# A fused attention and mixture-of-experts block on one core: expert weights in nine loads, block rows turned on VectorE, and a rewritten closing section

## The reference

```
gate = ki @ w0; hb = ki @ w2; hidden = silu(gate) * hb          # per head
w1g = newtonschulz5((hidden * lr1)^T vi)    # w0g, w2g alike: two rounds of X @ X^T, A @ A, B @ X
w_  = normalized(w_ + w_g)
oi  = silu(qi @ w0) * (qi @ w2) @ w1
```

```
gup = xf @ gate_up_proj[e] + 2 * (xf @ A^T) @ B^T               # 512 -> 2 * 256
h   = silu(gates) * h
out = h @ down_proj[e] + 2 * (h @ dA^T) @ dB^T                  # 256 -> 512
y   = sum of the two selected experts, weighted
```

## Time and profile before

| | us |
|---|---|
| median of 3 runs | 909.91 |
| the runs | 909.87, 912.17, 909.91 |
| the profiled execution, its own time | 913.66 |
| its span | 911.9 |
| PE / DVE / ACT busy | 849.4 / 646.5 / 644.4 |
| steady loop, one block | 5.81 |

### The profile page before, as it was taken

One profiled execution on the slowest core, in us unless ns is written; L12 is line 12 of the kernel. 1 busy time (PEld: TensorE's weight loads), 2 busy tenths in 40 slices (PEclk: granted clock), 3 DMA queues, 4 the chain that ended last, 5 costly groups with the idle time before them and its releaser, 6 DMA issues.

```text
span 911.9 us, 16072 instructions
## 1 busy us (share of the span) xinstructions
PE 849.4 (93%) x5128; PEld 525.9 (58%) x5128; DVE 646.5 (71%) x2315; ACT 644.4 (71%) x1417; POOL 347.0 (38%) x285
## 2 busy tenths in 40 slices
PE   6999999999999999999999999998899989999994
PEld 3657576575766757566575765756554434444442
DVE  2798989899898988989889898989735322222221
ACT  2878988888888988988888888887733323333331
POOL 2334344454444445344454444443132322222222
PEclk9999999999999999999999999999799999999998
DMA  9766426163351624426053250437334553444540
GB/s 329 269 208 175 117 93 176 49 195 88 123 148 66 206 60 150 117 93 187 23 164 102 85 140 19 111 92 296 158 72 70 125 92 62 84 84 80 84 73 0
DMA packets 56082, 110.98 MB, mean 122 GB/s; under 512 B 6576, under 2 KB 8240, under 8 KB 55360
## 3 DMA queue, kind: packets, MB, share of 16 engines
q1 hardware_dynamic: 47680, 92.84, 33.9%
q0 software_dynamic: 8176, 16.85, 9.8%
q10 hardware_dynamic: 144, 0.26, 0.1%
HBM read 47.22 MB, written 64.55 MB: 123 GB/s over the span
## 4 chain that ended last, share of the span: by engine, by line
PE 68%; DVE 14%; ACT 8%; DMA 4%; POOL 3%; issue 3%; SPq 0%; DVEq 0%; ACTq 0%; POOLq 0%
PE bank L128 17%; PE bank L134 10%; PE bank L1100 9%; PE bank L1121 5%; POOL t_small L2925 2%; PE bank L604 2%; PE bank L697 2%; DVE t_small L1598 2%; ACT t_arena L2506 1%; PE bank L641 1%; PE bank L609 1%; PE bank L636 1%; PE bank L627 1%; PE bank L677 1%; DMA xs_scratch<-t_arena 1%
## 5 line engine op out<-in xcount | busy, mean ns | idle before, releaser
L128 PEld LDWEIGHTS bank<-t_arena 128*128 128x128 bf16 (+1 forms) x1536 | 123.7, 123 | 112.7 <-issue 30.7
L128 PE MATMUL bank<-t_arena 128*128 128x128 bf16 (+1 forms) x1536 | 157.3, 238 | 16.0 <-ACT t_arena L2515 6.4
L134 PE MATMUL bank<-t_ident,t_arena 128*128 128x128 f32 x618 | 99.4, 282 | 14.0 <-DVE t_arena L1156 6.1
L134 PEld LDWEIGHTS bank<-t_ident,t_arena 128*128 128x128 f32 x618 | 72.3, 143 | 64.9 <-issue 37.8
L1100 PE MATMUL bank<-t_arena 128*128 x200 | 90.2, 594 | 2.4 <-ACT t_arena L2856 2.4
L3076 POOL DMA_INDIRECT out_x<-t_arena,t_tokx x25 | 38.6, 1546 | 111.7 <-DVE t_small L2226 101.6
L2847 ACT ACTIVATE t_arena<-bank 128x256 f32<-128x256 f32 x25 | 9.6, 383 | 78.0 <-PE bank L1100 78.0
L2229 DVE TENSOR_TENSOR t_arena<-t_arena,bank 128x256 f32<-128x256 f32 x25 | 10.5, 421 | 76.3 <-ACT t_arena L2847 76.3
L2931 POOL TENSOR_TENSOR t_small<-t_small,t_half 128x8 f32<-128x8 f32 x14 | 24.4, 1746 | 103.5 <-DVE t_small L1598 103.5
L1100 PEld LDWEIGHTS bank<-t_arena 128*128 128x128 f32 x200 | 35.9, 189 | 38.8 <-issue 38.8
L128 PE MATMUL bank<-t_W,t_arena 128*128 128x128 f32 x384 | 53.4, 282 | 0.7 <-ACT t_W L2416 0.2
(11 more groups left out here) (1097 smaller groups left out, 2322.9 us busy)
## 6 DMA issues: line engine op xcount, KB each, us to landing
xs_scratch<-t_arena SPq DMA_DIRECT2D x16, 2064.0 KB
t_arena<-xs_scratch SPq DMA_DIRECT2D x39, 258.0 KB, 2.7
t_arena<-in_gate_up SPq DMA_DIRECT2D x32, 256.0 KB, 3.6
wm_scratch<-t_arena SPq DMA_DIRECT2D x30, 256.0 KB
t_arena<-wm_scratch SPq DMA_DIRECT2D x5, 1536.0 KB, 11.0
t_arena<-in_wmod SPq DMA_DIRECT2D x5, 1024.0 KB, 10.4
t_arena<-in_down SPq DMA_DIRECT2D x16, 256.0 KB, 3.1
out_x<-t_arena SPq DMA_DIRECT2D x16, 256.0 KB, 2.0
```

The costliest lines, as they stand in the source:

```text
L128: mm = pe.matmul(bank[:, s], lhs[:, s], rhs[:, s], start=True, stop=True)
L134: mm = pe.transpose(bank[:, 128 * k:128 * k + 128], src[:, 128 * k:128 * k + 128], idn)
```

## The change

1. **Weights.** `expert(e, lo, hi)` loads part of an expert. There are nine transfers (four of 2048 columns, four of 1024, one of 3072). Three of 2048 columns stand ahead of chunk 14's output store on SP, each behind the last reader of its place: the products of chunk 14, and `m03`, `m13` of chunk 15's preparation. Block 0's "up" now waits for `s_e` 144.
2. **Rows.** `rows_in` loads a block in five transfers in place of one: four of 32 partitions x 4 pieces of 128 values (512 bytes each), which put the 32x32 squares where they belong, and one of 128x4 for the number, expert and weights (`xq`). DVE turns all sixteen squares in one instruction, and reads each square's columns four values apart; ACT reads SBUF, not a bank, for `xT`. PE's four transposes of each block are gone. The columns of the gate, the low-rank and the up weights are permuted outside the kernel to fit, so that the result is the same. `APPLY`'s transposes of h2 stay on PE, and take every fourth column (`h2k`).
3. **Order.** Chunk 15's section is written in a new order on all engines: the count of tokens per expert, its table and the output products of chunk 14 come first, chunk 15's forward products after them; up(0) to up(3) stand among the Newton-Schulz steps; up(13) stands before T(12); chunk 15's scatter stands behind block 8's in place of block 6's.

The core of the diff:

```
-        xg = cut(34820, 516, RING)
-        fs = cut(37916, 256, 2)
+        xg = cut(34820, 512, RING)
+        xgk = [r.rearrange("p (b i k) -> p b k i", b=4, k=4) for r in xg]
+        fs = cut(37892, 256, 2)
+        xr = arena[:, 38404:38916]
+        squares = xr.rearrange("p (b k j) -> p b k j", b=4, k=4)
...
-                turned(pe, A1, h2x, 4, ident[:, :]).then_inc(apply_pe, 1)
+                for k in range(4):
+                    mm = pe.transpose(A1[:, 128 * k:128 * k + 128], h2k[:, k, :], ident[:, :])
+                mm.then_inc(apply_pe, 1)
...
-                if t < NB:
-                    pe.wait_ge(s_g[t % RING],16 * (t // RING + 1))
-                    if t >= 1:
-                        pe.wait_ge(tn_act, nth(TN_ACT, t-1, "xT"))
-                    turned(pe, P0, xg[t % RING], 4, ident[:, :]).then_inc(tn_pe, 1)
...
-                    dve.wait_ge(s_g[t % RING],16 * (t // RING + 1))
+                    dve.wait_ge(s_g[t % RING],80 * (t // RING + 1))
+                    if t >= 1:
+                        dve.wait_ge(tn_act, nth(TN_ACT, t-1, "xT"))
+                    dve.transpose(xr, xgk[t % RING]).then_inc(tn_dve, 1)
...
+            def rows_in(sp, t, at):
+                for a in range(4):
+                    src = xs[bass.ds(at, 128), 128 * a:128 * a + 128].rearrange("(b j) n -> j b n", j=32)
+                    sp.dma_start(xg[t % RING][32 * a:32 * a + 32, :].rearrange("j (b n) -> j b n", b=4), src).then_inc(s_g[t % RING], 16)
+                sp.dma_start(xq[t % RING], xs[bass.ds(at, 128), 512:516]).then_inc(s_g[t % RING], 16)
...
             for c in range(NC - 1):
+                if c == NC - 2:
+                    sp.wait_ge(s_ms, 16 * STORED[NC - 1])
+                    for sem in (n0_pe, n1_pe, n2_pe):
+                        sp.wait_ge(sem, nth(N0_PE, c, "G"))
+                    sp.wait_ge(fwd_pe, len(FWD_PE) * (NC - 1))
+                    expert(7, 0, 2048)
+                    sp.wait_ge(prep_pe, nth(PREP_PE, NC - 1, "m03"))
+                    expert(0, 0, 2048)
+                    sp.wait_ge(prep_pe, nth(PREP_PE, NC - 1, "m13"))
+                    expert(2, 0, 2048)
```

And the head of the closing section on PE:

```
+            pe.wait_ge(mg_dve, nth(MG_DVE, NC - 2, "u0"))
+            pe.matmul(P0[:, 0:8], onesb[:, :], cum[(NC - 2) % 2][:, :], start=True, stop=True).then_inc(ta_pe, 1)
+            heads(pe, A0, W[0], qT[0]).then_inc(apply_pe, 1)
+            heads(pe, A1, W[2], qT[0]).then_inc(apply_pe, 1)
+            heads(pe, B0, kT[1], W[0]).then_inc(fwd_pe, 1)
```

More of the change, by code:

```diff
@@ L275, in adaln_block @@
         wx = [sm(1) for _ in range(RING)]
+        xq = [sm(4) for _ in range(RING)]
         full, ends, step8, done, rem, last = [sm(NE) for _ in range(6)]
@@ L962, in _ @@
             mm.then_inc(dn_pe, 1)
+            pe.wait_ge(apply_dve, nth(APPLY_DVE, NC - 1, "h2"))
+            for k in range(4):
+                mm = pe.transpose(A1[:, 128 * k:128 * k + 128], h2k[:, k, :], ident[:, :])
+            mm.then_inc(apply_pe, 1)
             pe.wait_ge(tn_act, nth(TN_ACT, 7, "xT"))
@@ L970, in _ @@
             turned(pe, CC(6), fs[0], 2, ident[:, :]).then_inc(dn_pe, 1)
-            pe.wait_ge(s_g[2], 32)
-            turned(pe, P0, xg[8 % RING], 4, ident[:, :]).then_inc(tn_pe, 1)
+            pe.wait_ge(apply_act, nth(APPLY_ACT, NC - 1, "h2T"))
+            for k in range(4):
+                q = slice(32 * k, 32 * k + 32)
+                mm = pe.matmul(A0[q, 0:128], gwm[:, k, :], h2T[:, 128 * k:128 * k + 128], start=True, stop=True)
+            mm.then_inc(apply_pe, 1)
             pe.wait_ge(dn_act, nth(DN_ACT, 6, "fT"))
@@ L1065, in _ @@
             mm.then_inc(dn_pe, 1)
-            pe.wait_ge(tn_act, nth(TN_ACT, NC - 3, "xT"))
-            for k in range(4):
-                mm = pe.matmul(AA(13)[:, :], xT[1][:, 128 * k:128 * k + 128],
-                               w_e[:, bass.ds(which[13], 1), 512 * k:512 * k + 512], start=(k == 0), stop=(k == 3))
-            mm.then_inc(up_pe, 1)
             pe.wait_ge(up_dve, nth(UP_DVE, NC - 3, "fs"))
@@ new lines, in _ @@
+            dve.tensor_tensor(last, ends, full, ALU.subtract).then_inc(tab_dve, 1)
+            dve.wait_ge(s_g[0], 240)
+            dve.wait_ge(tn_act, nth(TN_ACT, 11, "xT"))
+            dve.transpose(xr, xgk[12 % RING]).then_inc(tn_dve, 1)
+            dve.tensor_scalar(tokx[12 % RING], xq[12 % RING][:, 0:1].bitcast(U32), 2047, None, ALU.bitwise_and).then_inc(tn_dve, 1)
+            dve.tensor_scalar(wx[12 % RING], xq[12 % RING][:, 1:2], ebf[:, 12:12 + 1], xq[12 % RING][:, 2:3], ALU.is_equal, ALU.mult).then_inc(tn_dve, 1)
@@ L2638, in _ @@
-            act.wait_ge(n2_pe, nth(N2_PE, NC - 1, "AA0"))
-            act.copy(NTT[2], B2[:, :]).then_inc(n2_act, 1)
+            act.wait_ge(n2_pe, nth(N2_PE, NC - 1, "BX0"))
+            act.copy(NZT[2], B2[:, :]).then_inc(n2_act, 1)
+            act.wait_ge(tn_dve, nth(TN_DVE, 0, "tr"))
+            for k in range(4):
+                row = act.activation(xT[0][:, 128 * k:128 * k + 128].rearrange("p (b j) -> p b j", b=4), squares[:, :, k, :], ACT.Identity, scale=cb_c[:, k:k + 1], bias=sb_c[:, k:k + 1])
@@ L2842, in _ @@
                     act.copy(fT[b % 2], CC(b)[:, 0:256]).then_inc(dn_act, 1)
+                if t < NB:
+                    act.wait_ge(tn_dve, nth(TN_DVE, t, "tr"))
+                    if t >= 2:
+                        act.wait_ge(up_pe, nth(UP_PE, t-2, "up"))
+                    if t == 0:
+                        act.wait_ge(apply_pe, nth(APPLY_PE, NC - 2, "hq"))
+                    for k in range(4):
+                        row = act.activation(xT[t % 2][:, 128 * k:128 * k + 128].rearrange("p (b j) -> p b j", b=4), squares[:, :, k, :], ACT.Identity, scale=cb_c[:, k:k + 1], bias=sb_c[:, k:k + 1])
+                    row.then_inc(tn_act, 1)
                 if EB <= u < NB:
```

1354 lines of the change are left out of this document (666 added, 688 removed).

## The result

Twenty executions of each: 911.97 us median before, 908.55 us after; the ratio of the two is 0.997 with a 95% interval of 0.9958 to 0.9983, so 1.5 to 3.8 us faster. The forecast was 16.2 us faster, and the time lies outside 886 to 902.

The account below looks back on a forecast made before the run. PE's own work was taken to bound the loop. Closing section -6.0, boundary -0.15 and loop -10.0 gave -16.2: 913.66 to 897.5 for the profiled execution, 893.7 for the median, range 886 to 902.

Parts of the forecast that it names:

- The loop, -10.0: Blocks 16 to 38 lose PE's row turning, 23 x 0.436 = 10.0 us, if PE stays the bound at 5.38 us.
- When up(0) starts, 645.5, 7.0 earlier: Closing section: block 0's up starts at 645.5 in place of 652.48, with PE later than weights and rows.
- The chunks, taken as unchanged: Chunks up to 619 us: expected unchanged within 1 us.
- The 17.1: Closing section: 17.1 us from the last G (625.64) to its first product of round two (642.76), carried over to the new order.
- The reads: Ahead of up(0): fourteen reads of expert numbers on PE for nine, five more, partly in gaps, +1.7.
- The count: Start of PE's new order: it waits for chunk 14's last merge, 621.22 in place of 619.05, +2.2.
- The boundary, -0.15: From 750.65 to 758.75, ahead of the loop: 8.10 us become 0.22 + 3.44 + 1.1 + 3.2 = 7.95.
- Blocks 2 to 13, 98.2 unchanged: Stretch from up(0) to the loop: gains and moved chunk 15 steps set against each other, 98.2 us, plus or minus 4.
- Strided reads at nothing: Reads four values apart cost nothing extra; rival: twice as long, 7.0 us lost in the chunks, 900.7, chance 0.10.
- The DVE transpose, 0.70: In the loop: DVE's transpose of 128x512 takes 0.70 us likeliest, 0.6 to 1.36 as bounds, hidden under PE.
- The rivals: Three rivals: weights or rows bind up(0), 0.12; packets, not bytes, 0.08; strided reads by two 0.10, three 0.04, four 0.06.
- Packets, not bytes: Rival: the rows' DMA packets set the loop at 5.56 or more, 5.8 us saved for 10.0, 898 to 901, chance 0.08.

Follow-up runs that it names:

- experiment 3: The kernel before, with the rows of blocks 16 to 38 not turned at all, loads in one transfer as before: 907.01 us, ratio 0.9939.
- experiment 1: The changed kernel, with additions of odd blocks from 15 on going to a second tensor, each waiting only for its own tensor's: 905.41 us, ratio 0.9907.
- experiment 8: The changed kernel, with the three early weight loads of 2048 columns moved behind chunk 15's preparation: 909.05 us, ratio 0.9976.
- experiment 7: The changed kernel, with h2's four transposes in every chunk reading neighbouring columns in place of every fourth: 904.16 us, ratio 0.9928.
- experiment 6: The changed kernel, with only two expert numbers read ahead of up(0), and block b+2's number read behind up(b): 902.59 us, ratio 0.99.
- experiment 2: The changed kernel, with each row's 512 values loaded in one transfer of 128 packets from block 14 on: 909.91 us, ratio 0.9979.

## Why the prediction was wrong

Of 16.2 us forecast, 3.4 came by the medians, and 3.0 by the two profiles counted from the first merge products on. Three terms failed: up(0), by some 8.7 us, the loop, by 4.5 to 5, and the boundary, by 2.3. The second point below rests on three rows that are not shown above, the first of the timeline of PE before, the others of that of the changed kernel:

```profile
644.99 1.03 PE L128 MATMUL bank<-t_arena 128*128 128x128 bf16 x8
```

```profile
627.49 1.13 PE L128 MATMUL bank<-t_arena 128*128 128x128 f32 x8
...
649.51 0.63 PE L128 MATMUL bank<-t_arena 128*128 128x128 bf16 x4
```

- **The loop, -10.0.** The step that failed is "POOL's additions follow one another in 899.43 to 902.97, 3.54 us, also below 5.38". That distance is of blocks without tokens; a full block's is 5.68 with the old row load (experiment 3) and 5.78 with the new one. PE's own pace came as written, 5.37. From block 14's addition to block 38's the time fell from 136.80 to 131.76, 5.0 us, and that is what the loop gave; PE shows 7.86 less up to the last out and gives 2.31 back behind it. With nothing in the way (experiment 1) it is 126.27, 10.5 less, the size forecast. PE could run ahead while places of the ring were free, and waited once they were not.
- **When up(0) starts, 645.5, 7.0 earlier.** It was 649.94 in the profile, and counted from the first merge products 1.74 us later than before. The order read was right (PE's own chain, not weights or rows; experiment 8). What the sum had wrong:
  - *The chunks, taken as unchanged.* From the first merge products to chunk 14's pass 549.71 us for 545.67: 4.0 more, of which 1.5 comes of 39.05 a chunk for 38.94, 2.6 of the two chunks with the low clock (experiment 7).
  - *The 17.1.* It was read from two rows that do not belong together. 625.64 is the G of stream N1 (N0's stands at 626.56), but 642.76 is N0's last product of round one; N1's first product of round two is among those at 644.99, 19.35 behind its G. In the changed kernel the first G (N2's, 627.49) came 0.8 us behind the 626.7 forecast; N2's first product of round two follows at 649.51 and up(0) at 649.94. From that G to up(0) pass 22.45 us where 17.1 + 1.7 = 18.8 were allowed. 2.25 of the 3.65 missing are the row misread.
  - *The reads.* "Five more, partly in gaps: +1.7" is about right in size: twelve cost 4.2 us where they now stand, between the norm products (experiment 6), 0.35 each or 1.75 for five. What the nine cost in their old place no run measured.
  - *The count.* The +2.2 came as 2.84 (621.89 for 619.05). With the wait and the low clock the way from chunk 14's merge product to chunk 15's is 12.58 us for 11.42, and up to 15.2 in the experiments.
- **The boundary, -0.15.** "0.22 + 3.44 + 1.1 + 3.2" has the wait for xT(14) nearly right (3.2; 3.60 came), but takes up(14) at full clock. It took 5.30, and the boundary grew by 2.16. The wait itself was an order's fault, not a need: the rows of block 14 lay there, and turning them ahead of y(13) removed wait and slow product, some 5 us by the profile.
- **Blocks 2 to 13, 98.2 unchanged.** 98.17 before, 96.80 after: inside the 4 us allowed.
- **Strided reads at nothing.** 0.75 us for four transposes in place of 0.66, 0.09 us a chunk, 1.4 us in all, beside what the chunks with the low clock may add. The rival was priced from a factor of two, 7.0 us; the factor is 1.14. Here the Trainium skill, "SBUF — State Buffer", section "Door 1: The DMA port swizzle", by which accesses that each go to a new 16-byte line pay, points the right way, and the rows give the small size.
- **The DVE transpose, 0.70.** 1.10 us, inside its bounds and hidden in the loop. The estimate of 1.24 from the Trainium skill, "VectorE: DVE Perf Modes", section "The three transpose paths", was nearer.
- **The rivals.** None was the one that came. "Packets, not bytes" gave the right kind of end, a loop above 5.38 with late rows, by a wrong cause: experiment 2 takes the packets away and nothing changes. One argument for it misread its row, too: q0's packets are not the smaller ones, 16.85 MB in 8176 are 2.06 KB each, q1's 1.95. What would have told the right rival stood in the trace of before: the pair at 741.18 and 746.76.

How the experiments' medians split further was not measured; the start of an execution, the chunks with a low clock and the head of the closing section (12.6 us in the profiled execution of the changed kernel, 11.8 to 15.2 in the experiments with the same head) each vary from one profile of the same program to the next.

## What to carry to other kernels

Before an engine's work is taken out of a loop, price every other chain in it from rows in the middle of the loop, under the load it has there; the last iterations may be empty ones, and a chain that is waiting for the present bound shows only its wait, not its length. A chain's true period shows where two links touch, so look for the one row whose releaser is the link before. Instructions that an engine only issues (reads into registers) cost a third of a microsecond each here (4.2 for twelve) in a row of short dependent products; behind the long products of the loop, where one stands in every block, PE shows no gap. And before two profiles are subtracted, look how far apart they are before the change has begun to act: here 4.28 of the 7.3 us.
